# All 64 experts in the loop body, and five of eight picks read and added inside it: a transformer block with 64 routed experts on one core

## The reference, cut to what matters

```python
h = _layernorm(x, axis=-1) * (1 + ca) + sa
x = x + ga * _L0_attn_ref(h, ...)
h = _layernorm(x, axis=-1) * (1 + cb) + sb
x = x + gb * _L0_ffn_ref(h, ...)
# _L0_ffn_ref, x = h as 2048 rows:
logits = x @ gate_w.T
topv, topi = jax.lax.top_k(logits, TOP_K)            # 8 of 64
rw = jax.nn.softmax(topv, axis=-1)
W = jnp.zeros((N, E)).at[arange(N)[:, None], topi].set(rw)
gu = jnp.einsum('nh,eih->nei', x, gu_w)
gate, up = gu[..., :I], gu[..., I:]
inter_w = jax.nn.silu(gate) * up * W[:, :, None]
out = jnp.einsum('nei,ehi->nh', inter_w, dp_w)
out = out + sigmoid(x @ sh_gate1_w.T) * shared_expert(x)
```

## Time and profile before

| | |
|---|---|
| Runs before | 964.57, 967.36, 973.53 us (median 967.36) |
| Profiled execution, from the first to the last instruction | 965.6 us |
| Mean granted TensorE clock | 0.970 |
| TensorE / VectorE / GpSimd / ScalarE busy | 872.5 / 465.5 / 458.7 / 214.3 us |
| Moved by DMA | 221.36 MB, mean 229 GB/s |

### The profile page before, as it was taken

One profiled execution on the slowest core, in us unless ns is written; L12 is line 12 of the kernel. 1 busy time (PEld: TensorE's weight loads), 2 busy tenths in 40 slices (PEclk: granted clock), 3 DMA queues, 4 the chain that ended last, 5 costly groups with the idle time before them and its releaser, 6 DMA issues.

```text
span 965.6 us, 12358 instructions
## 1 busy us (share of the span) xinstructions
PE 872.5 (90%) x3437; PEld 514.2 (53%) x3437; DVE 465.5 (48%) x1177; ACT 214.3 (22%) x559; POOL 458.7 (48%) x447
## 2 busy tenths in 40 slices
PE   6999989989988694979989998999999999986997
PEld 2434534534534343657666665666666666763442
DVE  4797785788586540423323323333233333324496
ACT  2022221321312111212232222322223222321000
POOL 1420055236355766357556666566665656655000
PEclk9999999999998697989999999999999999998999
DMA  9951003103003152788898998889998997899997
GB/s 341 326 163 71 1 8 96 45 2 104 1 1 115 41 190 73 229 289 277 289 322 272 339 323 315 307 286 338 325 319 302 311 333 262 283 354 402 382 419 315
DMA packets 76927, 221.36 MB, mean 229 GB/s; under 512 B 19078, under 2 KB 19462, under 8 KB 76472
## 3 DMA queue, kind: packets, MB, share of 16 engines
q1 hardware_dynamic: 48760, 149.12, 43.9%
q0 software_dynamic: 28096, 71.42, 21.0%
HBM read 183.98 MB, written 48.87 MB: 241 GB/s over the span
## 4 chain that ended last, share of the span: by engine, by line
PE 60%; issue 8%; DVE 7%; another core or an unknown queue 7%; DMA 4%; SPq 3%; ACT 2%; ACTq 0%; POOL 0%; DVEq 0%; POOLq 0%
PE bank L2026 17%; PE bank L2046 8%; PE bank L1798 7%; PE bank L2016 5%; PE bank L1845 5%; PE bank L1911 3%; PE bank L2136 3%; DMA front<-y_rows 3%; PE bank L2037 2%; PE bank L1809 2%; SPq L668 2%; PE bank L2054 1%; PE bank L1930 1%; DMA front<-h_rows,gid_fixed 1%
## 5 line engine op out<-in xcount | busy, mean ns | idle before, releaser
L2026 PE MATMUL bank<-h2T,wqkv 128*128 128x256 f32 x1024 | 243.1, 388 | 9.9 <-issue 9.6
L719 POOL DMA_INDIRECT slot_table<-pair,place x128 | 130.4, 1019 | 183.3 <-DVE place L1262 118.2
L2026 PEld LDWEIGHTS bank<-h2T,wqkv 128*128 128x128 f32 x1024 | 193.1, 194 | 41.1 <-issue 16.5
L775 POOL DMA_INDIRECT y_rows<-front,tbl x110 | 113.6, 1033 | 83.8 <-DVE front L1641 38.1
L766 POOL DMA_INDIRECT front<-h_rows,gid_fixed x112 | 115.8, 1034 | 69.1 <-issue 31.6
L2046 PE MATMUL bank<-wqkv,front 128*128 128x512 f32 x256 | 127.9, 621 | 11.2 <-DVE front L1622 7.5
L1641 DVE TENSOR_SCALAR front<-bank,wgt 128x512 f32<-128x512 f32 x146 | 107.1, 748 | 43.3 <-DMA y_rows<-front,tbl 19.8
L1006 ACT ACTIVATE h2T<-bank 128x512 f32<-128x512 f32 x148 | 82.2, 595 | 161.4 <-issue 65.6
L1798 PE MATMUL bank<-wqkv,front 128*128 128x512 f32 x256 | 113.5, 594 | 0.0
L1622 DVE TENSOR_TENSOR front<-bank,front 128x256 f32<-128x256 f32 x64 | 27.2, 424 | 177.4 <-ACT front L1016 135.2
L2016 PEld LDWEIGHTS bank<-const,front 128*128 128x128 f32 x592 | 69.1, 143 | 62.0 <-issue 47.4
(11 more groups left out here) (292 smaller groups left out, 860.1 us busy)
## 6 DMA issues: line engine op xcount, KB each, us to landing
wqkv<-in_experts SPq DMA_DIRECT2D x64, 768.0 KB
front<-in_experts SPq DMA_DIRECT2D x36, 512.0 KB
front<-y_rows SPq DMA_DIRECT2D x20, 768.0 KB, 12.4
front<-in_experts SPq DMA_DIRECT2D x36, 256.0 KB
wqkv<-y_rows SPq DMA_DIRECT2D x12, 768.0 KB, 13.4
front<-in_w_mod SPq DMA_DIRECT2D x5, 1024.0 KB, 10.1
x<-in_x SPq DMA_DIRECT2D x4, 1024.0 KB, 10.8
h_rows<-h SPq DMA_DIRECT2D x4, 1024.0 KB
```

Source lines behind the costliest of these rows:

```text
L719: pool.indirect_dma_start(out=slots[:, :], out_offset=bass.IndirectOffsetOnAxis(ap=place[b % 2][:, i, k:k + 1], axis=0), in_=pair[:, b * T ...
L775: pool.indirect_dma_start(out=y_rows[:, :], out_offset=bass.IndirectOffsetOnAxis(ap=to, axis=0), in_=yb[s], in_offset=None, bounds_check=P ...
L2026: mm = pe.matmul(pair_bank[u % 2][:, j * PAIR:(j + 1) * PAIR], w[:, at:at + INNER], xT[u % 2][:, k, :], start=(k == 0), stop=(k == KC - 1))
```

## The change

- All 64 experts stand in the body, 128 tiles, with 18 single units after experts 13, 15, ..., 49 at the latest (`REST_AFTER`): 146 tiles, 82 units. There are no laps. What can't be placed goes to an overflow loop (`COLD`), entered only if its count is above zero; it is also entered if a token's picks lie too late for the early reads.
- Seven weight slots (`WSLOTS = 7`), nine for the first nine experts; slots 8 and 9 are then the half tiles' own.
- The half tiles' pair numbers are fetched from the slot table by GpSimd, one indirect DMA of 128 x 4 bytes for each single unit (`take_ids`), at addresses computed on VectorE. Their weights are picked by a comparison over the 64 router weights (`weight_picked`, VectorE). The register loads of VectorE and ScalarE in the body go; SyncE's stay.
- Five picks (7 to 3) are read in the loop, in chunks of four groups (1 MB), from the tile on by which experts 43, 50, 55, 58 and 60 are done. Pick 7 goes into 16 buffers; of the others each chunk goes into one of three sets of buffers and VectorE adds it in the loop (`add_next`, five tiles after the read); the last 12 additions stand in the final sums (`add_last`).
- Three picks (2 to 0) are read after the loop, one read of 768 KB a group, seven groups ahead; TensorE adds them.

```diff
-WSLOTS = 4
+WSLOTS = 7
+FIRST_SLOTS = 9
-REST_AFTER = [22 + 2 * (42 * m // 17) for m in range(REST)]
+REST_AFTER = [13 + (36 * m) // 17 for m in range(18)]
+SOON = 5
+EARLY_UPTO = [43, 50, 55, 58, 60]
 LATE = TOPK - EARLY
+CHUNK = 4
+ECHUNKS = 3
+CHUNK_AT = [EARLY_TILES[0] + 1 + 3 * i for i in range(CHUNKS)]
+CHUNK_AT += [EARLY_TILES[1] + 1 + 2 * i for i in range(CHUNKS)]
+CHUNK_AT += [EARLY_TILES[2] + 1 + 2 * i for i in range(CHUNKS)]
+CHUNK_AT += [EARLY_TILES[3] + 2 + i for i in range(2 * CHUNKS)]
-BACK = 5
+BACK = 7
...
+            def read_chunk(j):
+                k, c = j // CHUNKS, j % CHUNKS
+                landed_upto(sp, EARLY_TILES[k])
+                if k:
+                    n = j - CHUNKS
+                    if n >= ECHUNKS:
+                        sp.wait_ge(s_added, CHUNK * (n - ECHUNKS + 1))
+                    for i in range(CHUNK):
+                        sp.dma_start(next_row[CHUNK * (n % ECHUNKS) + i], y_view[CHUNK * c + i, :, TOPK - 1 - k, :]).then_inc(s_next[n % ECHUNKS], 16)
+                else:
+                    for i in range(CHUNK):
+                        sp.dma_start(early[CHUNK * c + i], y_view[CHUNK * c + i, :, TOPK - 1, :]).then_inc(s_first, 16)
+
+            for t in range(BODY_TILES):
                 e, n = BODY[t]
+                if e is not None and n == 1:
+                    if next_in_slot(e):
+                        sp.wait_ge(s_d, t + 1)
+                        load_fixed(next_in_slot(e))
+                    if e == FIRST_SLOTS:
+                        ...
+                        load_rest_gu(0)
+                        load_rest_down(0)
+                if t in REST_TILE[:-1]:
+                    n = REST_TILE.index(t)
+                    sp.wait_ge(s_G, REST_UNIT[n] + 1)
+                    load_rest_gu(n + 1)
+                    sp.wait_ge(s_d, t + 1)
+                    load_rest_down(n + 1)
+                for j in range(EARLY * CHUNKS):
+                    if CHUNK_AT[j] == t:
+                        sp.wait_ge(s_d, t + 1)
+                        read_chunk(j)
...
+            def take_ids(n):
+                pool.indirect_dma_start(
+                    out=sid_rest[:, n:n + 1], out_offset=None, in_=slots[:, :],
+                    in_offset=bass.IndirectOffsetOnAxis(ap=addr[:, n:n + 1], axis=0),
...
             for t in range(BODY_TILES):
...
+                for n in range(REST):
+                    if ID_AT[n] == t:
+                        take_ids(n)
                 if t >= STORE_BACK:
+                    put_rows(t - STORE_BACK)
+                if t + ROUND < BODY_TILES:
+                    gather(t + ROUND)
...
+            def weight_picked(u):
...
+                ve.scalar_tensor_tensor(out=picked[:, :], in0=const[:, C_PICK:C_PICK + EXPERTS], scalar=of,
+                                        in1=xg[s][:, D:XW], op0=ALU.is_equal, op1=ALU.mult,
+                                        accum_out=wgt[:, s:s + 1]).then_inc(s_picked, 1)
...
+            def add_next(m):
+                n, g = m // CHUNK, m % TILES
+                if m % CHUNK == 0:
+                    ve.wait_ge(s_next[n % ECHUNKS], 16 * CHUNK * (n // ECHUNKS + 1))
...
+                ve.tensor_tensor(early[g], early[g], next_row[m % (CHUNK * ECHUNKS)], ALU.add).then_inc(s_added, 1)
+            ADD_AT = [CHUNK_AT[CHUNKS + m // CHUNK] + SOON + m % CHUNK // 2 for m in range(CHUNK * ADDED)]
...
             for g in range(TILES):
+                ve.wait_ge(s_ft, g + 1)
+                step(t0, ve.tensor_tensor(early[g], early[g], sum_bank[g % BACK][:, :], ALU.add))
+                step(t0, ve.tensor_tensor(early[g], early[g], rows_g[:, g // TPB, :], ALU.mult))
+                ve.tensor_tensor(x_at(g), x_at(g), early[g], ALU.add).then_inc(s_fo, 1)
+                if TILES - CHUNK * ECHUNKS <= g + 3 < TILES:
+                    add_last(g + 3)
```

More of the change, by code:

```diff
@@ L1684, in _ @@
+                gated(u)
+                if u in LIST_REST_AT:
+                    list_rest(LIST_REST_AT.index(u))
+                taken(u)
+                while added < CHUNK * ADDED and ADD_AT[added] <= UNIT[u][-1]:
+                    add_next(added)
+                    added += 1
+            taken(UNITS)
+            while added < CHUNK * ADDED:
+                add_next(added)
+                added += 1
             used = laps_used(ve)
-            for r in range(OWN_LAPS):
-                lap(r)
```

1109 lines of the change are left out of this document (534 added, 575 removed).

## The result

The changed kernel took 1012.66 us (median of 4 runs) against 966.76 us for the kernel before in the same session: ratio 1.0444, 95% interval 1.0384 to 1.0504. It is slower by some 4%, where 1.6% faster was forecast. Run again on another chip (`a0`) it took 995.91 us where the kernel before took 958.6, a ratio of 1.039. The profile taken with the first result (1019.2 us) fell into a disturbed execution, so the profile read here is that of `a0`, with a span of 994.1 us.

What follows compares the result with a forecast made beforehand. TensorE and DMA were taken as level bounds. 361.3 before the loop, 110 start, 312 middle, 106 end and 61 tail sum to a 950 us span, 952 as median; range 935 to 965, or 922 to 976 without the outer tenths.

Steps and rivals of the forecast that it cites:

- I take 5: Start of the loop: of up to 19 us by which GpSimd's fetches exceed TensorE's pace, 5 us would show.
- part 4: The start of the expert loop, 13 pairs up to the first single: 110 us, from 104 to 122.
- at 2.0 lost for each single as before: Middle: 278 us of TensorE work plus 2.0 us lost per single unit, 312 in all.
- TensorE's 314 us against DMA's 313: Middle of the kernel before: TensorE work and DMA at full share are level, so relieving one alone buys little.
- Rival 3: From tile 102 on, early reads starve the gathers; 982 us, chance 0.12.
- 9 for the chunks and scatters: Pause after the last down: 9 us until the last early-read chunks and scatters are done, of 16.
- 5 for the first read and 2 for sum and handover: Rest of the 16 us pause: 5 for the first group's read to land, 2 for sum and handover.
- 43 us at 387 GB/s: Final sums: 16.8 MB at the last stretch's rate take 43 us, 12 less than the 55.1 before.
- the row against a rule: Tail: the trace's 387 GB/s was used, not the rule's 358, which would make the sum 4 us higher.
- Rival 1: Late semaphores go with the register loads, so middle 302, end 98, start 104; 928 us, chance 0.22.
- Rival 2: DMA takes the gain back: middle 325, end 113; 972 us, within 1% of before, chance 0.16.
- Rival 4: Overflow loop is entered after all, five picks read again; over 1000 us, chance 0.02.

Runs made afterwards that it cites:

- e4: Changed kernel with the 18 fetches of pair numbers spread, each 14 tiles ahead of its single unit; ratio 1.0296 to the kernel before.
- e7: Kernel before with 18 idle indirect DMAs of 128 x 4 bytes added on GpSimd at tiles 10 to 24; ratio 1.0233.
- b0: The kernel before, unchanged, profiled again on a third chip; 955.28 us, span 953.4.
- e8: Changed kernel with all scatters sent out of bounds, so issued but writing nothing; final reads take expert weights instead; ratio 1.0207.
- e9: Changed kernel with scatters not issued, an empty instruction signalling instead; final reads take expert weights; ratio 0.9565.
- e10: e5 with the half tiles' weight loads after the first single cut to 128 of 1536 columns; ratio 1.0146 to the kernel before.
- e1: Changed kernel with GpSimd issuing the gather of tile t+8 before the scatter of tile t-2; ratio 1.0262 to the kernel before.
- e11: e5 with the single tiles' router weight copied by ScalarE in place of the VectorE operation; ratio 1.0165 to the kernel before.
- e12: e5 with TensorE signalling a pair unit's two down products once, behind the second; ratio 1.0160 to the kernel before.
- e13: e5 with the scatter of tile t-3 in place of t-2 beside the gather of tile t+8; ratio 1.0084 to the kernel before.
- e15: e5 with GpSimd held once in each pair unit until the silu of the unit before is done; ratio 1.0153 to the kernel before.
- e6: Changed kernel with four early picks' reads and additions cut to 8 of 512 columns; ratio 1.0237 to the kernel before.
- e5: Changed kernel with fetches of pair numbers spread and gathers ahead of scatters on GpSimd; ratio 1.0203 to the kernel before.

## Why the prediction was wrong

**The start: the failed step is "I take 5" in part 4.** The sum there was right, 24 us of fetches and 19 over TensorE's pace, and then 14 of the 19 were called hidden behind the gathers' lead and the scatters' buffers. Measured: the start took 126.7 against 110; spreading the fetches gave 15.6 back (e4), and adding them to the kernel before lengthened its start by 10 (e7, with 13 of the 18 in it). So 10 to 16 us were paid where 5 were allowed. They were not paid in the way the sum had it, by gathers that come late: TensorE waited for gathers about as long with the fetches (11.6 us) as without (12.1 in b0, 14.1 in e4). Some 11 of e4's 15.6 us are the two gate/up products that took 11.3 and 9.7 us. So the sum lacked a term, what TensorE itself loses while GpSimd issues the added fetches without a gap. Why it loses it, and why e7, with runs as long, shows no slow product, is open.

**The middle: "at 2.0 lost for each single as before" failed.** It was 3.0 a single, 329.4 for 312, against 2.0 and 1.2 in the two profiles of before. The prediction weighed TensorE's 314 us against DMA's 313 and called these the two bounds. GpSimd, busy 210.7 us of 348.1, was left out; e8, e9 and e10 show that the middle answers to its issuing, and that DMA was not the second bound there. The order of its queue, which the edit turned and the prediction did not see, is 11 us of the whole (e1), 4 of them here. Why the changed kernel then loses 1 to 2 us more a single than before, with gathers first and fetches spread, stays open. It is not that GpSimd has more to issue: 184 indirect DMAs in the 329.4 us of a0's middle are fewer to the microsecond than 205 in 348.1 or 203 in 334.5 before. They lie otherwise: 15 runs of nine or more without a gap in a0, nine in each profile of before. Nor is it the weights' engine (e11), the number of signals (e12) or the load traffic (e10). The scatters' place gave 8 us of the whole (e13), a wait in GpSimd's queue none (e15), and neither broke the runs. Long runs and more singles to the pair are candidates that were not tried by themselves.

**The end (106 forecast, 107.2) was right, in part by luck:** 6 us of it are the turned order (e1), for which the forecast had no term, and 7.5 the early reads (e6). e1's end ran at 375 GB/s over 101 us, with the share at 1.00, and lost 9.6 us over its bare 91.8. Rival 3's place was there, and it cost little: TensorE waited 0.6 us for gathers, VectorE 11.4 us for chunks, and before the last down TensorE 4.4 us for VectorE.

**The pause: 16 was forecast, 24.3 measured.** "9 for the chunks and scatters" was 14, "5 for the first read and 2 for sum and handover" was 10. The timeline of SyncE, then of VectorE:

```profile
926.50 0.32 SPq L680 DMA_DIRECT2D qsin<-y_rows  x1
...
934.56 0.60 SPq L680 DMA_DIRECT2D qcos<-y_rows  x1
...
940.76 10.34 SPq L729 DMA_DIRECT2D store<-y_rows  x8
```

```profile
950.86 0.69 DVE L1740 TENSOR_TENSOR wo<-wo,bank 128x512 f32<-128x512 f32 x1 [17.74 <-PE bank L2177]
```

The last three chunks go out from 926.5 on, beside and behind the last down (926.6), the last scatters land among them, the first final read is issued 14 us after the last down, with more reads right behind it, and its sum starts 10 us later. With the chunks cut to 8 columns the pause is 16.4 (e6): the early reads' tail is these 8 us.

**The tail's sums were right in size, 43.2 for 45, but not by the bound named.** The sum had DMA first, 43 us at 387 GB/s. The stage moved 309 GB/s at a share of 0.77, since seven of its 16 reads had been issued in the pause; VectorE was busy 39.2 us of it and TensorE 38.5, near the 41 that the prediction had for each. On bandwidth the prediction went by the row against a rule. The Trainium skill, page "DMA: Bandwidth & Descriptors", section "Bandwidth", has the HBM side bind at about 358 GB/s for a core; the same section gives about 358 as the share of a core when both cores of the HBM domain stream, and this kernel runs on one. This case's rows again stand above it, 375 GB/s in e1's end and 401 in b0's pause.

**The rivals.** Rival 1 is false: the register loads of ScalarE and VectorE went, and the unnameable waits grew from 102 us in b0's middle to 152 in a0's. Rival 2 had the middle and end near their size (325 and 113) for a reason that e10 refutes. Rival 3 had the right sign and the wrong mechanism. Rival 4 did not occur: after the last down there is one short pause and no repeated read. The outcome lay outside the range: no case had GpSimd's issuing as what sets the pace, though the prediction had written down 4.0 us of its time a tile against TensorE's 3.03. Of the 41 us between a0 and b0 the experiments put some 10 to 16 on the fetches and 11 on the order, and what is left in e5, whose ratio is 1.020, is mostly open.

## What to carry to other kernels

Give the engine that issues indirect DMAs a line of its own in the balance of each stretch, instructions times their length, also where its busy share is 60%: here emptying its scatters of bytes gave 6 us in the middle and not issuing them 36 more. When an edit adds such instructions, spread them: the same 18 fetches, moved apart, gave 15.6 us back in the start and added none that shows in the middle. And check what the waits of the kernel before are before you read one as a sign: those for gathers in the start were there without the fetches. Last, compare the order of every queue line by line before forecasting: a swap of two lines that the description does not mention was worth 11 to 20 us.

## What was not expected of the hardware

An indirect DMA of GpSimd takes 1.0 us and 0.3 to the next whether it moves 128 rows of 2 KB, 128 x 4 bytes, or nothing. ScalarE and VectorE waited up to 10.5 us for signals of TensorE products that had ended, while GpSimd was issuing, and most of the long waits in a0's middle ended 1.0 to 1.5 us behind GpSimd's last indirect DMA before a gap; with GpSimd's busy time in the middle at 93 us instead of 190 they were on time. And TensorE's own matmuls, 0.22 us apart elsewhere in a gate/up product, came 0.7 to 1.4 us apart for a while beside the two longest runs of a0, at 440 and 471 us. What holds them is not settled by these runs.
